# Attention inside a macaron layer: the far key blocks' relative term as four rows of the stacked queries and keys

## What is computed

```python
x = x + 0.5 * ffn(layernorm(x))      # two of 8 experts and a shared one
x = x + attention(layernorm(x))      # 16 sequences of 512 rows, 16 heads of 8
x = x + 0.5 * ffn(layernorm(x))
# attention:
dist = clip(arange(s)[:, None] - arange(s)[None, :], -128, 128) + 128
scores = einsum('bhqd,bhkd->bhqk', q, k) + einsum('bhqd,qkd->bhqk', q, rel_emb[dist])
attn = softmax(scores / sqrt(8)); local = attn @ v
# beside it a global term from elu(q) + 1, M and z; gate mixes the two; then @ Wo.T + bo
```

## Time and profile before

| | |
|---|---|
| time, median of 3 runs | 2408.51 us (2407.59 to 2410.61) |
| the profiled execution's own time | 2397.57 us |
| its span | 2395.8 us |
| busy: PE, PEld, DVE, ACT, POOL | 86%, 60%, 63%, 59%, 48% of the span |
| HBM read and written | 193 GB/s over the span |
| mean granted clock of TensorE | 0.93 |
| chain that ended last | 5% PE, 4% POOL, 4% ACT, 4% DMA: the end of the second FFN |

### The profile page before, as it was taken

One profiled execution on the slowest core, in us unless ns is written; L12 is line 12 of the kernel. 1 busy time (PEld: TensorE's weight loads), 2 busy tenths in 40 slices (PEclk: granted clock), 3 DMA queues, 4 the chain that ended last, 5 costly groups with the idle time before them and its releaser, 6 DMA issues. The chain is left out here.

```text
span 2395.8 us, 49346 instructions
## 1 busy us (share of the span) xinstructions
PE 2062.3 (86%) x16104; PEld 1439.5 (60%) x16104; DVE 1517.0 (63%) x4212; ACT 1422.2 (59%) x2771; POOL 1161.2 (48%) x1524
## 2 busy tenths in 40 slices
PE   4667899769999999999999999999999777799950
PEld 3556677535666666566666666666666566577640
DVE  7775556546767776776766666666664676556641
ACT  3655666536666666666666667666665455566640
POOL 0776004346665656555644545455441177400676
PEclk9888999959999999999999999999999788999985
DMA  5356877668887888878878888887883014577862
GB/s 132 127 198 207 246 242 251 197 188 234 224 232 230 240 236 237 239 215 232 240 206 235 241 235 232 230 235 229 237 242 100 26 50 157 179 249 237 273 206 74
DMA packets 294450, 492.50 MB, mean 206 GB/s; under 512 B 43956, under 2 KB 198452, under 8 KB 294196
## 3 DMA queue, kind: packets, MB, share of 16 engines
q1 hardware_dynamic: 238324, 308.21, 45.5%
q0 software_dynamic: 53248, 180.01, 23.8%
q10 hardware_dynamic: 2624, 1.13, 0.2%
HBM read 252.56 MB, written 210.89 MB: 193 GB/s over the span
## 5 line engine op out<-in xcount | busy, mean ns | idle before, releaser
L1414 DVE CUSTOM_DVE_ANT_0 at_junk<-at_ps_s,at_rel 128x512 bf16<-128x512 f32 x1024 | 664.6, 686 | 261.6 <-PE at_ps_s L980 204.3
L1153 ACT ACTIVATE at_probs<-at_ps_t 128x512 f32<-128x512 f32 x1024 | 558.6, 597 | 112.6 <-PE at_ps_t L965 96.7
L1162 ACT COPY at_src<-at_ps_r 128x512 f32<-128x512 f32 x512 | 302.3, 590 | 363.8 <-PE at_ps_r L992 266.1
L965 PE MATMUL at_ps_t<-tab_ident,at_rel 128*128 128x128 f32 x3328 | 490.4, 287 | 0.0
L965 PEld LDWEIGHTS at_ps_t<-tab_ident,at_rel 128*128 128x128 f32 x3328 | 366.5, 144 | 70.3 <-issue 3.4
L509 POOL DMA_INDIRECT rows_x<-ffn_xe,rows_index x256 | 262.4, 1025 | 182.2 <-ACT ffn_xe L461 106.2
L519 POOL DMA_INDIRECT ffn_zg<-rows_z,rows_home x176 | 176.8, 1004 | 348.1 <-issue 348.1
L1006 PE MATMUL at_ps_v<-at_probs,at_v 128*32 128x256 f32 x4096 | 333.5, 398 | 0.2 <-ACT at_probs L1153 0.2
L720 DVE TENSOR_TENSOR ffn_h<-ffn_silu,ffn_ps_gate 128x512 f32<-128x512 f32 x248 | 170.4, 687 | 255.5 <-ACT ffn_silu L482 254.9
L980 PE MATMUL at_ps_s<-at_ks,at_qs 24*128 24x512 f32 x1024 | 308.6, 508 | 5.8 <-DVE at_mx L1414 3.8
L482 ACT ACTIVATE ffn_silu<-ffn_ps_mid 128x512 f32<-128x512 f32 x248 | 148.6, 599 | 239.3 <-PE ffn_ps_gate L321 239.2
(11 more groups left out here) (203 smaller groups left out, 3430.8 us busy)
## 6 DMA issues: line engine op xcount, KB each, us to landing
at_band<-at_src POOLq DMA_DIRECT2D x192, 574.0 KB, 4.9
at_rel<-at_band SPq DMA_DIRECT2D x512, 143.5 KB, 4.3
ffn_w_expert<-rows_w SPq DMA_DIRECT2D x92, 768.0 KB, 4.9
at_band<-at_src POOLq DMA_DIRECT2D x64, 512.0 KB
ffn_xg<-rows_x SPq DMA_DIRECT2D x92, 256.0 KB, 3.9
rows_z<-ffn_y SPq DMA_DIRECT2D x92, 256.0 KB, 5.2
rows_x<-ffn_zero SPq DMA_DIRECT2D x46, 256.0 KB
at_rel<-at_band SPq DMA_DIRECT2D x64, 128.0 KB
```

The costliest lines, as they stand in the source:

```text
L965: ins = pe.matmul(ps_t[:, i, HALF * n + P * l:HALF * n + P * (l + 1)], rel[:, c % RREL, l, 2 * hp + i, kb * P:(kb + 1) * P], ident[:], sta ...
L1153: act.activation(probs[:, kp, 2 * hp + i].rearrange("p n q -> p (n q)"), ps_t[:, i, :], ACT.Exp).then_inc(exp_done.sem, 1)
L1162: act.copy(src[:, l, 2 * hp:2 * hp + 2, 0:BAND], ps_r[:, :, 0:BAND]).then_inc(qr_out.sem, 1)
L1414: dve.tensor_tensor_reduce(out=junk[:, i, :], in0=ps_s[:, i, :], in1=rel[:, c % RREL, l, h, :], scale=1.0, scalar=-3e38, op0=ALU.add, op1= ...
```

## The change

For a query and head, the value that a far block on the right needs is q times one vector: (rel_emb for "128 or more after") minus (the one for "128 or more before"), scaled. The change makes it for all heads of a sequence by one product with a weight of 16 columns, splits it into high and low, and stacks it into four new rows of qs (two for query blocks 0, 2 and two for 1, 3; high and low). The matching rows of ks are fixed: 0 for key blocks in reach of the band and 1 for those beyond it. So both score products have it (rows 24 to 28 and 25 to 29), rel is zero there, and transposes and fills stop at key block qb+1.

```diff
+    FAR = 4
+    FAR_PROJECT, FAR_OUT, FAR_IN = (3, 3), (4, 0), (4, 1)
@@ scores_turned, add_turned, scores (PE)
-                    rows = slice(32 * h, 32 * h + ROW + 1)
+                    rows = slice(32 * h, 32 * h + ROW + FAR + 1)
-                            if kb < qb - 1:
+                            if kb < qb - 1 or kb > qb + 1:
                                 continue
+                if k == 0 and c % PER == 0:
+                    far_ring, n = seq_ring(far_in, c // PER)
+                    pe.wait_ge(far_ring.sem, far_ring.at(n + 1, 0))
...
-                    rows = slice(32 * h, 32 * h + ROW)
+                    rows = slice(32 * h, 32 * h + ROW + FAR)
@@ turn_maximum (PE)
+                elif slot == 4 and b is not None:
+                    pe.wait_ge(far_done.sem, far_done.at(b, 2))
@@ project (PE)
+                elif place == FAR_PROJECT:
+                    pe.wait_ge(qhi_done.sem, qhi_done.at(b, 1))
+                    pe.wait_ge(qlo_done.sem, qlo_done.at(b, 1))
+                    pe.wait_ge(v_done.sem, v_done.at(b, 1))
+                    maximum_left(c)
+                    if e is not None:
+                        pe.wait_ge(g_step.sem, g_step.at(e, 6))
+                    for i, (w, q) in enumerate(((wf_hi, q_hi), (wf_hi, q_lo), (wf_lo, q_hi))):
+                        ins = pe.matmul(misc[0:H, 0:HALF], w[:], q[:, 0:HALF], start=(i == 0), stop=(i == 2))
+                    ins.then_inc(far_prod.sem, 1)
@@ leave, TURN_MIXED (PE)
+                    if coming(c) is not None:
+                        pe.wait_ge(far_done.sem, far_done.at(coming(c), 2))
@@ project (ACT, q_hi), x_out (ACT), project (POOL, q_lo)
+                    far_prod.wait(act, b, 0)
+                far_ring.wait(act, n + 1, 0)
+                    far_prod.wait(pool, b, 0)
@@ before the slots (ACT)
+            act.wait_ge(cleared.sem, 1)
+            for x in range(FAR):
+                to = bass.AP(qs[:].tensor, (ROW + x) * LINE, [[32 * LINE, HG], [1, LINE]])
+                act.dma_start(to.bitcast(F32), local[:, 0, :]).then_inc(plain_in.sem, 16)
@@ fill_far (POOL)
-                        pool.tensor_copy(rel[:, c % RREL, l, :, key:S],
-                                         far[:, c % RREL, l].broadcast_to([P, HG, S - key])).then_inc(fill_done.sem, 1)
+                        end = P * (2 * half_of(c) + l + 2)
+                        pool.tensor_copy(rel[:, c % RREL, l, :, key:end],
+                                         far[:, c % RREL, l].broadcast_to([P, HG, end - key])).then_inc(fill_done.sem, 1)
@@ before the slots (POOL)
+            pool.memset(local[:, 0:3, :], 0.0).then_inc(cleared.sem, 1)
+            pool.memset(glob[:, 2:4, :], 1.0).then_inc(cleared.sem, 1)
@@ stack (SP)
+                if place == FAR_IN:
+                    sp.wait_ge(far_done.sem, far_done.at(b, 2))
...
+                    for x in range(FAR):
+                        l, part = x // 2, x % 2
+                        at = (ROW + x) * LINE + r * SETS * S + P * l
+                        to = bass.AP(qs[:].tensor, at, [[32 * LINE, HG], [S, SETS], [1, P]])
+                        src_at = HALF * part + P * l
+                        sp.dma_start(to.bitcast(F32), xT[0:H, src_at:src_at + P]).then_inc(far_ring.sem, 16)
@@ before the slots (SP)
+            for x in range(FAR):
+                near = HALF + P * (x // 2)
+                for plain, low, high in ((local[0:32, 0:near // P, :], 0, near), (glob[0:32, 2:2 + (S - near) // P, :], near, S)):
+                    to = bass.AP(ks[:].tensor, (ROW + x) * LINE + low, [[32 * LINE, HG], [S, R2 * SETS], [1, high - low]])
+                    sp.dma_start(to.bitcast(F32), plain).then_inc(extra_in.sem, 16)
@@ project (DVE)
+                elif place == FAR_OUT:
+                    high, low = (xT[0:H, HALF * part:HALF * (part + 1)].bitcast(F32R) for part in range(2))
+                    dve.wait_ge(far_prod.sem, far_prod.at(b, 1))
+                    dve.tensor_copy(high, misc[0:H, 0:HALF]).then_inc(far_done.sem, 1)
+                    dve.wait_ge(far_done.sem, far_done.at(b, 1))
+                    dve.tensor_tensor(low, misc[0:H, 0:HALF], high.bitcast(F32), ALU.subtract).then_inc(far_done.sem, 1)
@@ V_OUT of the first sequence (DVE), for j = 0 and 2
+                                dve.memset(rel[:, j, 0, :, 2 * P:S], 0.0).then_inc(rel_cleared.sem, 1)
                                 dve.memset(rel[:, j, 1, :, 0:P], 0.0).then_inc(rel_cleared.sem, 1)
+                                dve.memset(rel[:, j, 1, :, 3 * P:S], 0.0).then_inc(rel_cleared.sem, 1)
```

More of the change, by code:

```diff
@@ L843, in attention_phase @@
         misc = ps("misc", [P, S])
-        step, stats_done, eps_set, rstd_done, cleared, rel_cleared, minus_in, pads_in = (
-            ring(x, 0) for x in ("step", "stats_done", "eps_set", "rstd_done", "cleared", "rel_cleared", "minus_in", "pads_in"))
+        step, stats_done, eps_set, rstd_done, cleared, rel_cleared, extra_in, pads_in = (
+            ring(x, 0) for x in ("step", "stats_done", "eps_set", "rstd_done", "cleared", "rel_cleared", "extra_in", "pads_in"))
         late_added, late_step = ring("late_added", 1), ring("late_step", 1)
@@ L856, in attention_phase @@
         k_in = [[ring(f"k_in{r}{hp}", 16 * PART * 2) for hp in range(2)] for r in range(R2)]
+        far_in = [ring(f"far_in{r}", 16 * FAR) for r in range(R2)]
+        far_prod, far_done, plain_in = ring("far_prod", 1), ring("far_done", 2), ring("plain_in", 0)
         bo_done = ring("bo_done", 1)
@@ L1407, in maximum @@
                     if c == 0:
-                        dve.wait_ge(cleared.sem, 3)
-                        dve.wait_ge(rel_cleared.sem, 6)
+                        dve.wait_ge(cleared.sem, 5)
+                        dve.wait_ge(rel_cleared.sem, 10)
                 for i in range(2):
@@ L1479, in leave @@
                         y_prod.wait(dve, b, 0)
+                        if b == 0:
+                            dve.wait_ge(plain_in.sem, 16 * FAR)
+                            dve.wait_ge(extra_in.sem, 16 * (2 * FAR + 1))
                     dve.wait_ge(o_step.sem, o_step.at(b, 2 * p + 1))
@@ L1588, in table_scratch @@
     scratch.rel = sb("rel", [P, NREL])
-    scratch.rel_left = sb("rel_left", [P, 1])
+    scratch.rel_left, scratch.rel_right, scratch.rise = (sb(x, [P, 1]) for x in ("rel_left", "rel_right", "rise"))
+    scratch.far_of = sb("far_of", [P, io["head_of"].shape[1]])
     scratch.near = sb("near", [P, NREL - 1])
@@ L1597, in table_scratch @@
     scratch.m_gated = sb("m_gated", [P, io["M"].shape[1]])
-    scratch.scaled, scratch.split_rel, scratch.picked, scratch.gated = (
-        signal(x) for x in ("scaled", "split_rel", "picked", "gated"))
+    scratch.scaled, scratch.split_rel, scratch.picked, scratch.gated, scratch.spread = (
+        signal(x) for x in ("scaled", "split_rel", "picked", "gated", "spread"))
     return scratch
@@ L1609, in table_steps @@
     if u == 0:
+        dve.tensor_scalar(scratch.rise[:], scratch.rel_right[:], scratch.rel_left[:, 0:1], SCALE, ALU.subtract,
+                          ALU.mult).then_inc(scratch.spread, 1)
         dve.tensor_scalar(wk[:], wk[:], SCALE, None, ALU.mult)
@@ L1630, in table_steps @@
                                  in1=scratch.chosen[:], op0=ALU.mult, op1=ALU.add)
+        dve.wait_ge(scratch.spread, 1)
+        dve.tensor_scalar(scratch.far_of[:].rearrange("p (h s) -> p h s", h=4),
+                          scratch.head_of[:].rearrange("p (s h) -> p h s", h=4), scratch.rise[:, 0:1], None,
+                          ALU.mult).then_inc(scratch.spread, 1)
     elif u == 5:
+        dve.wait_ge(scratch.spread, 2)
+        dve.tensor_copy(tables.wf_hi[:], scratch.far_of[:]).then_inc(scratch.spread, 1)
         dve.tensor_scalar(scratch.gate1[:], gate[:, 1:2], 1.0, None, ALU.add).then_inc(scratch.gated, 1)
@@ L1637, in table_steps @@
     elif u == 6:
+        dve.wait_ge(scratch.spread, 3)
+        dve.tensor_tensor(tables.wf_lo[:], scratch.far_of[:], tables.wf_hi[:].bitcast(F32), ALU.subtract)
         dve.tensor_scalar(tables.wv[:], tables.wv[:], gate[:, 2:3], None, ALU.mult)
@@ L1664, in load_phase @@
             (to[:], io[name]) for to, name in (
-                (scratch.rel, "rel"), (scratch.rel_left, "rel_left"), (scratch.part_of, "part_of"), (scratch.z_sb, "z"),
+                (scratch.rel, "rel"), (scratch.rel_left, "rel_left"), (scratch.rel_right, "rel_right"), (scratch.part_of, "part_of"), (scratch.z_sb, "z"),
                 (scratch.head_of, "head_of"), (tables.ident, "ident"), (tables.wk, "wk"), (tables.bk, "bk"),
@@ L1796 @@
         "rel": rel[::-1].T[p % 32 // 3 % 8],
+        "rel_right": rel[0][p % 32 // 4].reshape(128, 1),
         "rel_left": rel[-1][p % 32 // 4].reshape(128, 1),
```

28 lines of the change are left out of this document (18 added, 10 removed).

## The result

The changed kernel takes 2449.5 us (median of 4 runs, 2439.8 to 2455.3) against 2409.6 of the kernel before in the same comparison: ratio 1.0163, 95% interval 1.0126 to 1.0199. It is slower by 40 us. I had forecast 2388 and a range up to 2425.

What follows compares the result with a forecast made beforehand. PE was taken to bound the steady attention, with SP's queue second in slots 2 to 5. Slots 0 and 6 -24, stretch +6.4, last sequence -4, start +1.5: -20.1 us, from 2408.51 to 2388; range 2343 to 2425.

Steps and rivals of the forecast that it cites:

- Early ones (eight): Slots 2 to 5 of eight early sequences: 2.8 us of room takes up much of the added DMAs; -0.6 us each.
- 2.4 us for four issues: SP's queue in slot 4, ahead of slot 5's fetch and maximum: four far DMAs add 2.4 us per sequence.
- -0.8 us of gaps: SP's queue, slots 2 to 5: shorter POOL fills remove SP's 0.77 us wait for a fill, credited as -0.8 us.
- Slots 0 and 6: Fewer transposes on PE save 1.3 us in slot 0 and 0.3 in slot 6: 15 x -1.6 = -24 us.
- the band's way: Slots 6 to 7: the band's landing doesn't get shorter, so ACT's wait grows; slot 6 gains 0.3 us, not 0.54.
- the last sequence: Last sequence has no stacking: 48 transposes fewer, 5.2 us at PE's price, taken as -4 us.
- the stretch: SP's work in slots 2 to 5: seven late sequences +1.6 us each, eight early ones -0.6, sum +6.4 us.
- C: Rival: SP's added DMAs lengthen all 15 stretches, 36 us; slots 0 and 6 give -12; +21.5, 2430 us; chance 0.19.
- B: Rival: PE sets the time everywhere and SP's issues are absorbed; 4.2 us saved per sequence, 2341 us; chance 0.15.
- The other rule: An issuing engine's solid DMA track means DMA-bound: every sequence's stretch would get longer by all of the 2.4 us.
- The start: Before the attention: eight more SP DMAs, four on ACT, clearings on DVE, table steps; 0 to 5 us, taken as +1.5.
- Costs taken as nothing: PE's far product, four more score rows, the far_done wait and DVE's two steps, covered by other waits: 0 us.

Runs made afterwards that it cites:

- second group: Far DMAs issued by ACT in the changed kernel: 1.0004; DMAs added to the kernel before: four in slot 0 0.9992, two in slot 4 1.0099, four one-row 1.0193.
- fourth group: Granted-clock runs: kernel before without far transposes of slots 0, 2, 4 but with slot 6's, 0.9930; changed kernel with slot 6's zero-block transposes redone, 1.0122; and variants.

## Why the prediction was wrong

**The step that failed first: "Early ones (eight): if they had no room either, +1.6 as well; if the 2.8 us of room take up all of it ... I take -0.6".** The term was -0.6 us a sequence, and +3.3 came: the room did not take up the DMAs. Slot 5 grew as much in early sequences as in late ones, by 3.3 and 3.2 us (means of 7 each, 10.71 to 13.97 and 11.47 to 14.70). The 6.63 us from SP's issue to PE's turn were PE's own steps, and the scores that need the maximum came without a wait. In the kernel before:

```profile
767.62 0.51 PE L952 MATMUL at_ps_t<-at_qs,at_ks 25*128 25x256 f32 x4
```

In the changed kernel SP's issue came so much later in PE's work that PE waited 4.20 us there, and the distance became 7.86. The runs with added DMAs alone cost early sequences 1.3 to 1.9 us less than late ones (second group), near the 2.2 us by which I had set them apart, but from a much higher cost: 2.8 us early and 4.1 late for four. Why the changed kernel shows no such difference, no run here says.

**The same term's price.** 2.4 us for four issues was right as issue time (2.26 in the timeline) and too small as a cost: 47 us in the run with four added, over 15 sequences 3.1 us each. As a mean over 14 sequences, SP's way from the maximum of item 3 to that of item 6 grew from 36.2 to 38.9 us, and the way from there to PE's turn from 5.3 to 6.0, 3.4 us together. The -0.8 us of gaps that I had credited to the fills did not show: the pair of runs without and with short fills gave 0.9972 and 0.9970. In the sequence of the earlier trace rows the gap did close, but the six groups of fetches took 15.7 us instead of 14.0. Part of what is above 2.3 us is the clock behind the longer wait, 3.0 us lost in slot 5 against 0.45; how much of the time that makes I did not separate, since the run with four added has the same 14.5 us in slot 5 with 1.4 us lost.

**Slots 0 and 6, "15 x -1.6 = -24".** Slot 0 gave 0.8 of the 1.3 us: 10.16 to 9.40. Slot 6 gave 0.3 where nothing else held it (8.68 to 8.37 with fewer transposes), as taken. But slot 7, which I had not priced at all, took 1.1 us back in both kernels. I had named a cause for slot 7, the band's way, and limited it to what slot 6 saves. Where transposes alone were left out it was for the most part the clock, as the fourth group shows. In the changed kernel the clock was part of it: slot 7's lost clock grew by 0.6 us (0.37 to 0.96), and PE's wait there for ACT's copies of bands from 0.08 to 0.47 us, which is the cause that I had named, though ACT's own wait for bands hardly grew over the attention (81.3 to 83.3 us). Together with the last sequence, at most 7 to 10 us came of the 28 (ratios 0.9972 and, with everything but the DMAs, 0.9959).

**Sum as measured:** the change without the DMAs 0.9959, so -10 us; the four DMAs from there to 1.0163, so +49; together +40 (the two steps come from different comparisons). The forecast had -28 +6.4 +1.5. Of the 60 us between -20 and +40, the stretch makes 43 (about 18 by the early sequences' -0.6 in place of +1.6, 25 by the price), and the small gains make the rest.

**The rivals.** C was right as told, in its mechanism and its sign: added DMAs in all sequences, halved gains, DVE's wait for rel up by 33 us. Its price was too low: 36 us for the DMAs where 49 came, -12 for slots 0 and 6 where slot 7 left little. B failed on its first sentence, that SP's issues would be absorbed. The Trainium skill (DMA: Bandwidth & Descriptors, Issuing engines are not separate DMA queues) calls the time to initiate a DMA usually small relative to the DMA. The trace agrees as far as that goes, 0.57 us for the maximum's DMA, for which PE's wait ended 2.45 us after the issue began; but small was not free, and 0.54 to 0.59 us for one row or sixteen decided the outcome. The other rule that I had weighed, that of the Trainium skill (Perfetto Trace Analysis, What "DMA-bound" means), would have given 2.4 us in every sequence; that was nearer than my discount.

**The start** cost 2.9 us where I had taken 1.5. The pads, issued behind eight DMAs more, took 6.14 us on SP instead of 2.65:

```profile
484.12 0.72 SPq L1439 DMA_DIRECT2D at_ks<-at_local  x1
...
490.25 6.14 SPq L1444 DMA_DIRECT2D at_band<-at_glob  x4
496.44 1.65 SPq L940 DMA_DIRECT2D at_qs<-at_q_hi  x2
```

**Costs taken as nothing** (PE's product, four more rows, the wait for far_done, DVE's two steps) held as far as the runs can tell: with all of them and without the DMAs the ratio was 0.9959, and with none of them, in the kernel before with fewer transposes and short fills, 0.9970.

## What to carry to other kernels

Count a DMA by the time that its issue takes from its queue at that place, not by its bytes, and look for a place where the queue idles or another engine can issue it: the same four cost 47 us in slot 4 and none in slot 0. At that place four issues more cost their full price while four fewer gave nothing, so a distance between two events is not slack until a run has shown it. And before taking work off PE, look at the granted clock of the stretch behind: here slot 6 saved 0.3 us by its missing transposes, and slot 7 took 1.1 us more.

## What was unexpected of the hardware

Leaving out transposes brought the mean granted clock from 0.97 to 0.93, and the loss stood in the slot behind the thinned one: in the windows above PE was busy for 7.78 of 8.17 us, and then had 1.2 GHz for a part of slot 7. Eight transposes took 1.97 us at that level and 1.09 at 2.4 GHz. With the transposes of slot 6 done again, both windows show 1.00. The Trainium skill (TensorE: Matmul & The Clock Gate, Part 4: PE-mode transpose) says that such transposes don't count as PE being busy in the same way. Here the clock stayed at the upper level with them, beside the products between them, and fell without them; what part of that is the transposes themselves and what the longer slot, no run separates.

An issue on SP took 0.59 us (median) for a single row of 512 bytes and 0.54 for sixteen such rows, and 0.54 on ACT for sixteen.

The kernel before took 6% longer in some comparisons than in others, and the difference lies outside the attention: in the first FFN 217 and 190 GB/s and a clock of 0.93 and 0.89, first the kernel before as profiled at the start, then the run with four DMAs in slot 0:

```profile
100.00:480.00 380.00, 310.49 (x1521) 240.94 (x1519) 236.08 (x505) 224.34 (x476) 150.76 (x148) 0.93 0.67 217
```
```profile
100.00:540.00 440.00, 335.38 (x1576) 258.67 (x1576) 246.79 (x537) 235.10 (x501) 151.49 (x148) 0.89 0.59 190
```

Why, no run here shows. That it is the chip is not shown either: three comparisons name the same chip number, and before took 2557, 2400 and 2554 us in them.
